# Two cross-attention layers on one core: third score group written behind the second, four maxima a layer, inverse root in eight steps, engines in another order

## Chip, cores and metric

The kernel runs on one core of a Trainium2 chip. The metric is the device time of one execution in microseconds, the median over several runs. The core has five engines with an instruction stream each: PE (TensorE, matrix products; PEld are its weight loads), DVE (VectorE), ACT (ScalarE), POOL (GpSimd) and SP (SyncE, which here issues all transfers). Products land in PSUM, eight banks of 512 floats on each of 128 partitions; an engine waits for another on semaphores.

## What is computed

Two cross-attention layers in turn, on 64 batches of 256 positions and 320 channels, 20 heads of 16. Layer 0 attends to 77 text tokens. Layer 1 attends to 73 text tokens and, with another softmax, to 4 image tokens, whose scores are raised by the cosine between what the head has read from the text and each image token. Cut to what matters:

```python
# layer 0
q, k, v = heads(x @ Wq.T), heads(text @ Wk.T), heads(text @ Wv.T)
x = merge(softmax(q @ k.T * D ** -0.5) @ v) @ Wo.T + bo + x
...
# layer 1
probs_t = softmax(q @ k_t.T * D ** -0.5)
text_out = probs_t @ v_t
qsem = l2norm(probs_t @ text_ehs)
fused = q @ k_ip.T * D ** -0.5 + 0.5 * (qsem @ l2norm(ip_ehs).T)
ip_out = (softmax(fused) * spatial_mask) @ v_ip
x = merge(text_out + ip_out) @ W_out + b_out + x
```

## The kernel before, in words

A first part (`keys_and_values`) computes keys, values and Gram matrices of all batches and stores them to HBM. The second part (`attention`) is a software pipeline over the 64 batches, written out in full: iteration i runs, on each engine, a fixed list of steps, and the step `1u3/4` is step u, part 3, of layer 1 for batch i-4. The lists are the strings of `ORDER`, one for each engine; nothing else sets the order. An engine works through its list strictly in that order, so a step that waits holds all behind it.

One batch and layer takes these steps; the engine is in brackets. q: query projection in high and low half-precision parts (PE, then ACT `q_high`, DVE `q_low`). s: scores with queries on the partitions, only to find their maxima (PE `scores`, L958 and L965; DVE `maxima`, L1184). The 20 heads lie in three groups of columns: two of 8 heads (c = 0, 1) and a third of 4 (c = 2). m: the maxima turned (PE L974, ACT `mt`). t: the scores again, with tokens on the partitions and the maximum subtracted by a product with a selector `sel` (PE `turned_scores`, L997 and L1000; ACT exponentials L1122). a: probabilities times values (PE L1017; ACT reads the sums, L1130). o: output projection (PE L933, L936; DVE L1277). Layer 1 alone has h and b (the exponentials split in two, ACT and POOL), u (times the Gram matrix, PE L1033), w (DVE L1206), n (square norms, PE L1045, ACT `nst`), i (image scores, PE L1061, ACT L1148), y (the image softmax, 21 short DVE steps L1224 to L1259 with one exponential on ACT, step f, L1154) and p (image attention, PE L1071, DVE L1266). xh and xl (POOL) split the input of a layer. SP moves the norms through HBM (ns, nl) ahead of y, the probabilities (ps, pl) ahead of p, inverse denominators (rw, rl) and numerators (sh) ahead of the step `at` of POOL.

PSUM is shared out by the table `USES`: one line for each bank, with the uses that follow one another in it. `Turns.wait` makes the first instruction of a use wait until the use before it in each of its banks has been read. Units are numbered by pairs of banks: the scores of group c go to units s2c and s2c+1, and the third group has a use of its own, s4, over four banks. In the same way t4 is the third group of the turned scores, over four banks; y is a work area of the image softmax, in one bank.

```python
uses = [f"s{2 * c}", f"s{2 * c + 1}"] if c < 2 else ["s4"]
wait_free(pe, l, b, *uses)
```

The inverse root of y is three Newton steps of three instructions each behind a bit trick of two.

Of the kernel before, what the change touches and what calls it, by code (L numbers as in the profile page):

```python
# [151 lines left out]
]  # L152
# [521 lines left out]
def attention(nc, psum, early, x, k_dram, v_dram, g_dram, c_dram, kip_dram, vip_dram, r_dram, n_dram, s_dram, p_dram,  # L674
# [3 lines left out]
    with ExitStack() as stack:  # L678
# [487 lines left out]
        def _(dve):  # L1166
# [3 lines left out]
            def maxima(l, b, n):  # L1170
# [6 lines left out]
                b.reached(dve, f_s[l], CW, c + 1)
                if n < 4:
                    o = banks(l, f"s{n}", 2)[:, :, 0:4 * m].rearrange("p r (x t) -> p r x t", t=m)
                    dst = mneg[l][:, 2 * half:2 * half + 2, 2 * c:2 * c + 2, :].rearrange("p j x s -> p j (x s)")  # L1180
                else:
                    o = banks(l, "s4", 4)[:, :, 0:2 * m].rearrange("p r (x t) -> p r x t", t=m)
                    dst = mneg[l][:, :, 4:6, 0]
# [24 lines left out]
            def ip_softmax(l, b, k):  # L1208
# [7 lines left out]

                newton = 3
                last = newton + 3 * NEWTON
                if k:
                    b.reached(dve, s_y, STEPS, k)  # L1220
                if k == 0:
                    wait_free(dve, l, b, "y")
                    b.reached(dve, s_nl, 16, 16)
# [3 lines left out]
                elif k == 2:  # L1227
                    ins = dve.tensor_scalar(y.bitcast(I32), y.bitcast(I32), -1.0, float(MAGIC), ALU.mult, ALU.add)
                elif k < last:
                    turn, part = divmod(k - newton, 3)  # L1230
                    if part == 0:
                        ins = dve.tensor_tensor(sy[:], y, sq[:], ALU.mult)
                    elif part == 1:
                        ins = dve.tensor_tensor(sy[:], y, sy[:], ALU.mult)
                    else:
                        ins = dve.scalar_tensor_tensor(y, sy[:], -3.0 * SCALES[turn] ** 2, y, ALU.add, ALU.mult)
# [259 lines left out]
```

## Time and profile before

| | us |
|---|---|
| median of 3 runs | 2527.18 (2525.49 to 2535.39) |
| profiled execution, its own time | 2528.66 |
| its span | 2526.9 |
| PE busy | 2294.1 (91%) |
| DVE busy | 1702.7 (67%) |
| ACT busy | 1709.4 (68%) |
| POOL busy | 1596.7 (63%) |

Busy times are of the whole span; the first part of the kernel takes the first sixth of it. A span is the time from the first to the last instruction of the trace. In the order of time each row gives a start in us from the start of the span, a length, the engine, the line of the kernel, what is written and read, a count, and in brackets how long the engine was idle before it and what released it; "issue" stands where the trace shows no releaser.

### The profile page before, as it was taken

What the parts mean: (1) busy time and instruction counts of PE and PEld (TensorE: products, weight loads), DVE (VectorE), ACT (ScalarE), POOL (GpSimd) and SP (SyncE); (2) the same over time, 40 slices, a digit from 0 to 9 for tenths busy, and PEclk for the clock granted to TensorE, in tenths of its full rate; (3) what the DMA queues carried; (4) which work ended last, traced back from release to release, by engine and by line L of the source; (5) the groups of instructions that cost most, each with busy time, mean ns of one, the idle gap of its engine ahead of it and who ended that gap; (6) DMA issues with size and microseconds to landing.
All of it is one profiled execution on the core that took longest, in us unless ns stands there. A gap on an engine that the chain in (4) does not pass through costs nothing.

```text
span 2526.9 us, 90581 instructions
## 1 busy us (share of the span) xinstructions
PE 2294.1 (91%) x35896; PEld 1472.0 (58%) x35896; DVE 1702.7 (67%) x3052; ACT 1709.4 (68%) x2602; POOL 1596.7 (63%) x1056
## 2 busy tenths in 40 slices
PE   7899958999989999999999999999999999999974
PEld 5677735555555555555555555555555555555542
DVE  5534424777777777777777777777777777777763
ACT  3323326777777777777777777777777777777762
POOL 3212134767777777777777776777777776777663
PEclk9999979999999999999999999999999999999997
DMA  9678632444433343344444444343443434444331
GB/s 286 196 222 236 198 106 57 111 111 112 114 107 108 112 114 110 108 116 111 116 116 116 116 113 110 107 114 109 113 115 112 111 110 111 116 115 116 109 88 54
DMA packets 337789, 310.90 MB, mean 123 GB/s; under 512 B 180208, under 2 KB 280816, under 8 KB 337392
## 3 DMA queue, kind: packets, MB, share of 16 engines
q1 hardware_dynamic: 337392, 305.36, 42.7%
q8 instruction: 280, 4.59, 0.8%
q14 instruction: 117, 0.96, 0.1%
HBM read 164.66 MB, written 105.98 MB: 107 GB/s over the span
## 4 chain that ended last, share of the span: by engine, by line
PE 51%; DVE 9%; ACT 8%; issue 7%; DMA 4%; SPq 4%; POOL 2%; ACTq 0%; DVEq 0%; POOLq 0%
PE psum L933 18%; PE psum L1017 8%; PE psum L1033 8%; PE psum L997 5%; ACT ef L1122 5%; PE psum L936 4%; DVE mneg L1184 4%; PE psum L965 2%; DVE x L1277 2%; PE psum L1071 2%; PE psum L1000 2%; DMA x<-in_x 2%; SPq L862 2%; ACT ust L1130 1%; DVE q_low L1191 1%
## 5 line engine op out<-in xcount | busy, mean ns | idle before, releaser
L1122 ACT ACTIVATE ef<-psum 73x1024 f32<-73x1024 f32 (+1 forms) x640 | 624.5, 1016 | 265.0 <-PE psum L1000 264.1
L1345 POOL TENSOR_TENSOR e<-ef,eh 73x1024 f32<-73x1024 f32 x320 | 679.1, 2131 | 179.3 <-PE psum L1045 128.3
L1184 DVE TENSOR_REDUCE mneg<-psum 128x8 f16<-128x584 f32 (+1 forms) x640 | 465.0, 775 | 138.3 <-PE psum L958 76.4
L1206 DVE TENSOR_TENSOR e<-psum,e 73x1024 f32<-73x1024 f32 x320 | 385.5, 1205 | 92.3 <-PE psum L1033 92.3
L1017 PE MATMUL psum<-ef,values 128*32 128x256 f32 x5120 | 345.0, 387 | 15.8 <-ACT ef L1122 10.8
L1033 PE MATMUL psum<-eh,gram 128*73 128x512 f16 x1280 | 333.3, 386 | 13.2 <-DVE x L1277 1.1
L997 PE MATMUL psum<-q_high,keys 32*73 32x256 f16 (+2 forms) x6144 | 325.1, 259 | 21.6 <-ACT ef L1122 19.1
L1137 ACT ACTIVATE eh<-ef 73x1024 f16<-73x1024 f32 x320 | 329.4, 1049 | 1.6
L1307 POOL TENSOR_TENSOR ust<-ust,rb 128x768 f32<-128x768 f32 x128 | 233.2, 1822 | 102.8 <-DMA ust<-ust 83.4
L1312 POOL TENSOR_TENSOR al<-ust,ah 128x768 f16<-128x768 f32 x128 | 210.1, 1641 | 89.5 <-ACT ah L1160 89.5
L1130 ACT ACTIVATE ust<-psum 128x512 f32<-128x512 f32 x384 | 215.1, 595 | 75.4 <-PE psum L1017 75.3
L997 PEld LDWEIGHTS psum<-q_high,keys 32*73 32x73 f16 (+1 forms) x6144 | 181.4, 110 | 127.2 <-issue 42.0
L933 PE MATMUL psum<-ah,wo 128*128 128x256 f16 x1280 | 194.6, 275 | 32.3 <-issue 19.6
L1302 POOL TENSOR_TENSOR xl<-x,xh 128x768 f16<-128x768 f32 x127 | 209.1, 1647 | 19.0 <-POOL xh L1295 0.9
L1017 PEld LDWEIGHTS psum<-ef,values 128*32 128x32 f32 x5120 | 135.6, 109 | 130.1 <-issue 31.1
L1295 POOL CAST xh<-x 128x768 f16<-128x768 f32 x127 | 104.7, 824 | 161.0 <-DMA x<-in_x 116.9
L1000 PE MATMUL psum<-mt,sel 32*73 32x256 f16 (+3 forms) x3072 | 202.7, 251 | 0.0
L997 PE MATMUL psum<-q_low,keys 32*73 32x256 f16 (+3 forms) x3072 | 202.6, 251 | 0.0
L1191 DVE SCALAR_TENSOR_TENSOR q_low<-psum,q_high 128x640 f16<-128x640 f32 x128 | 104.7, 818 | 142.8 <-ACT q_high L1104 142.8
L1033 PEld LDWEIGHTS psum<-eh,gram 128*73 128x73 f16 x1280 | 123.8, 115 | 120.6 <-DVE x L1277 26.7
L1045 PE MATMUL psum<-e,pick 128*32 128x256 f32 x2560 | 166.7, 389 | 1.2 <-DVE e L1206 1.2
L1089 ACT ACTIVATE res<-x,bias 128x256 f32<-128x256 f32 x320 | 140.9, 499 | 39.0 <-DVE outt L1277 24.1
(165 smaller groups left out, 4439.1 us busy)
## 6 DMA issues: line engine op xcount, KB each, us to landing
rb<-r_dram SPq DMA_DIRECT2D x128, 384.0 KB, 3.8
keys<-k_dram SPq DMA_DIRECT2D x128, 231.0 KB, 4.1
values<-v_dram SPq DMA_DIRECT2D x128, 192.5 KB
x<-in_x SPq DMA_DIRECT2D x64, 384.0 KB, 3.3
ust<-ust SPq DMA_DIRECT2D x512, 48.0 KB, 2.4
v_dram<-vst SPq DMA_DIRECT2D x64, 320.0 KB
out<-outt SPq DMA_DIRECT2D x64, 320.0 KB, 2.2
k_dram<-kst SPq DMA_DIRECT2D x32, 616.0 KB, 3.9
```

The costliest lines, as they stand in the source:

```text
L933: mm = pe.matmul(o[:, c * S:(c + 1) * S], a, data[:, k, :], **at_ends)
L997: pe.matmul(o, keys(l, low, c)[rows, e, 0:n], q[rows, cols], start=(low == 0 and q is qh[l]), stop=False)
L1000: mm = pe.matmul(o, sel[rows, 2 * c + e, 0:n], mt[l][rows, 0:many], start=False, stop=True)
L1017: mm = pe.matmul(row(l, f"a{c}")[j * SLOT:(j + 1) * SLOT, r * S:(r + 1) * S], va[l][:, h, :], e, start=True, stop=True)
L1033: mm = pe.matmul(banks(l, f"u{k}", 2)[0:n, r, :], gm[:, half, :], e, start=(half == 0), stop=(half == 1))
L1122: act.activation(ef[l][0:m, unit_heads(n), :].rearrange("t h s -> t (h s)"), src, ACT.Exp, scale=SM).then_inc(s_exp[l], 1)
L1130: act.activation(ust[l][:, b.parity(), :, c, :], src, ACT.Copy).then_inc(s_u[l], 1)
L1137: act.activation(eh[0:m, unit_heads(k), :], ef[1][0:m, unit_heads(k), :], ACT.Copy, scale=0.5)\
L1184: dve.tensor_reduce(dst, o, AX_X, ALU.max, negate=True).then_inc(s_max[l], 1)
L1206: dve.tensor_tensor(rest, banks(l, f"u{k}", 2)[0:m, :, :], rest, ALU.mult).then_inc(s_wr, 1)
L1307: pool.tensor_tensor(at(l, b), at(l, b), rb[l][:], ALU.mult).then_inc(s_at[l], 1)
L1345: pool.tensor_tensor(e2[0:m, k, :, :], ef[1][0:m, unit_heads(k), :], eh[0:m, unit_heads(k), :], ALU.subtract).then_inc(s_e2, 1)
```

## The change

The third group of scores loses its own step and its own banks. It is issued right behind the second (c = 1), into columns 4n to 6n of the same four banks. So there are two score steps a layer instead of three, and four maxima instead of five: two of 2 x 2 columns of heads and halves, then two of 2 x 3. The maxima of the third group lie elsewhere in `mneg`, and the selector product picks them with another row of `sel` and, for the second half, from other columns of `mt`; number and size of the products are the same.

The inverse root is one cubic step of five instructions and one Newton step of three, eight for nine. The wait for the bank of y moves from its first instruction, which doesn't touch the bank, to the second.

All five orders and the bank table are new. In the new table 1i shares a bank with 0a2 and 1u3; y shares one with 0a1; 0o takes banks of t4; 1o's bank goes to 0t1, the second unit of 0t0.

```diff
-RD_READ = 4 + 3 * NEWTON
+MAXIMA = 4
+CUBIC = 8.0 / 3
+ROOT_STEPS = 8
+RD_READ = 4 + ROOT_STEPS
...
 ORDER = {
...
     "dve": """
...
+        1y11/4 1y12/4 1y13/4 1y14/4 1y15/4 1y16/4 1y17/4 1y18/4 1y19/4 1ql/2 1s0/2 1s1/2 1s2/2 1s3/2 1w3/3
...
 USES = [
...
+    "0a1/1 1u3/3 0q/0 0s3/0 1t4/2 1y/3",
...
-    READ = {"q": ("ql", 1, 1), "s": ("max", UNITS, None), "m": ("mt", 1, 1), "t": ("exp", UNITS, None),
+    READ = {"q": ("ql", 1, 1), "s": ("max", MAXIMA, None), "m": ("mt", 1, 1), "t": ("exp", UNITS, None),
...
-                uses = [f"s{2 * c}", f"s{2 * c + 1}"] if c < 2 else ["s4"]
+                uses = [f"s{2 * c}", f"s{2 * c + 1}"]
...
-                if c == 2:
-                    for j in range(NJ):
-                        rows = slice(j * SLOT, (j + 1) * SLOT)
-                        o = banks(l, "s4", 4)[:, j, 0:2 * n].rearrange("p (e t) -> p e t", e=2)
-                        mm = pe.matmul(o, qh[l][rows, 2 * S:PW], keys(l, 0, c)[rows, :, 0:n], start=True, stop=True)
-                    mm.then_inc(f_s[l], 1)
-                    return
...
+                if c == 1:
+                    for j in range(NJ):
+                        rows = slice(j * SLOT, (j + 1) * SLOT)
+                        o = banks(l, uses[j // 2], 2)[:, j % 2, 4 * n:6 * n].rearrange("p (e t) -> p e t", e=2)
+                        mm = pe.matmul(o, qh[l][rows, 2 * S:PW], keys(l, 0, 2)[rows, :, 0:n], start=True, stop=True)
                 mm.then_inc(f_s[l], 1)
...
-                        mm = pe.matmul(o, sel[rows, 2 * c + e, 0:n], mt[l][rows, 0:many], start=False, stop=True)
+                        k, lead = (2 * c + e, 0) if c < 2 else (2 * c, e * many)
+                        mm = pe.matmul(o, sel[rows, k, 0:n], mt[l][rows, lead:lead + many], start=False, stop=True)
...
+                many = 2 + c
+                o = banks(l, f"s{n}", 2)[:, :, 0:2 * many * m].rearrange("p r (x t) -> p r x t", t=m)
+                dst = mneg[l][:, 2 * half:2 * half + 2, 2 * c:2 * c + many, :].rearrange("p j x s -> p j (x s)")
                 dve.tensor_reduce(dst, o, AX_X, ALU.max, negate=True).then_inc(s_max[l], 1)
...
+                cubic, newton = 3, 8
+                last = newton + 3
...
+                if k == 1:
+                    wait_free(dve, l, b, "y")
...
+                elif k in (cubic, newton):
+                    ins = dve.tensor_tensor(sy[:], y, sq[:], ALU.mult)
+                elif k == cubic + 1:
+                    ins = dve.tensor_tensor(fs, y, sy[:], ALU.mult)
+                elif k == cubic + 2:
+                    ins = dve.scalar_tensor_tensor(sy[:], fs, -10.0 / 3, sy[:], ALU.add, ALU.mult)
+                elif k == cubic + 3:
+                    ins = dve.tensor_tensor(sy[:], y, sy[:], ALU.mult)
+                elif k == cubic + 4:
+                    ins = dve.scalar_tensor_tensor(y, sy[:], 5.0, y, ALU.add, ALU.mult)
```

Three places of the order, line numbers of each kernel its own (the new one's stand a few lines lower or higher).

First PE, from the image attention of layer 1 (1p) to its output projection (1o), before: L965 and L958 are scores of layer 0 (0s0, 0s1, 0s2), L1045 the square norms, L997 the first rows of the turned scores 1t1 and 1t2, L1033 is 1u0, L1017 is 1a0.

```order
L1071 MATMUL psum<-pt,vb 128x256 x3
L1045 MATMUL psum<-e,pick 32x256 x8
L965 MATMUL psum<-keys,q_high 128x2x77 x8
L1045 MATMUL psum<-e,pick 32x256 x12
L965 MATMUL psum<-keys,q_high 128x2x77 x8
L997 MATMUL psum<-q_high,keys 73x256 x4
...
L1033 MATMUL psum<-eh,gram 73x512 x4
L997 MATMUL psum<-q_high,keys 73x128 x4
...
L1017 MATMUL psum<-ef,values 32x256 x8
L958 MATMUL psum<-keys,q_high 128x154 x4
L933 MATMUL psum<-ah,wo 128x256 x4
```

And of the change:

```order
L1069 MATMUL psum<-pt,vb 128x256 x3
L1043 MATMUL psum<-e,pick 32x256 x12
L957 MATMUL psum<-keys,q_high 128x2x77 x8
L1043 MATMUL psum<-e,pick 32x256 x8
L957 MATMUL psum<-keys,q_high 128x2x77 x8
L963 MATMUL psum<-keys,q_high 128x154 x4
L994 MATMUL psum<-q_high,keys 73x256 x4
...
L1031 MATMUL psum<-eh,gram 73x512 x4
L1015 MATMUL psum<-ef,values 32x256 x8
L994 MATMUL psum<-q_high,keys 73x128 x4
...
L932 MATMUL psum<-ah,wo 128x256 x4
```

0s0 stands behind three square-norm units instead of two, the third group directly behind 0s1, and 1a0 ahead of 1t2.

Second PE, from the first score step of layer 1 (1s0, L965) to the Gram product 1u3 (L1033), before: between them 0a1, 1s1, then 1a2 and 0a2 (x8 together), the third group 1s2 (L958) and the image scores 1i (L1061).

```order
L965 MATMUL psum<-keys,q_high 128x2x73 x8
L1017 MATMUL psum<-ef,values 32x256 x8
L965 MATMUL psum<-keys,q_high 128x2x73 x8
L1017 MATMUL psum<-ef,values 32x256 x8
L958 MATMUL psum<-keys,q_high 128x146 x4
L1061 MATMUL psum<-q_high,kipb 32x256 x2
...
L1033 MATMUL psum<-eh,gram 73x512 x4
```

And of the change:

```order
L957 MATMUL psum<-keys,q_high 128x2x73 x8
L1015 MATMUL psum<-ef,values 32x256 x12
L957 MATMUL psum<-keys,q_high 128x2x73 x8
L963 MATMUL psum<-keys,q_high 128x146 x4
L1059 MATMUL psum<-q_high,kipb 32x256 x2
...
L1015 MATMUL psum<-ef,values 32x256 x4
L1031 MATMUL psum<-eh,gram 73x512 x4
```

0a2 now stands with 0a1 (x12) ahead of 1s1, and 1a2 behind 1i.

Third DVE, from the read of 0o (written to x) to the low query part of layer 1 (q_low), the change alone:

```order
L1279 SCALAR_TENSOR_TENSOR x<-psum,res 128x768
...
L1226 TENSOR_TENSOR sy<-psum,sq 96x64
L1236 TENSOR_TENSOR sy<-psum,sy 96x64
L1238 SCALAR_TENSOR_TENSOR psum<-sy,psum 96x64
L1201 TENSOR_TENSOR e<-psum,e 73x1024
L1241 SCALAR_TENSOR_TENSOR psum<-psum,rd 96x64
L1244 SCALAR_TENSOR_TENSOR psum<-den,psum 96x256
...
L1254 TENSOR_REDUCE psum<-psum 96x64
...
L1261 TENSOR_TENSOR pip<-psum,fm 96x256
L1186 SCALAR_TENSOR_TENSOR q_low<-psum,q_high 128x640
```

Before, the whole inverse root stood ahead of the read of 0o, around the read of 1o, and only the eight steps from the product with `den` on behind it; now seven more short steps stand behind it, the product 1w2 between them, and the read of 1o stands behind the first step alone.

## Rows read from the trace of the kernel before

**Rows 1.** Busy time by stretch: length, busy us (instructions) of PE, PEld, DVE, ACT, POOL; PEclk, DMA

```profile
1300.00:1600.00 300.00, 281.10 (x4708) 175.06 (x4699) 223.10 (x397) 229.20 (x339) 215.81 (x148) 1.00 0.41 114
```

**Rows 2.** One line's instructions (image attention, step 1p), whole run: first and last start

```profile
L1071 PE MATMUL psum<-pt,vb x384: 374/478/789, 465.2 to 2514.0; 32*128 32x256 f32 x192
```

**Rows 3.** Order of time on PE, one period: start, length, instructions, idle before and releaser

```profile
1303.58 0.61 PE L933 MATMUL psum<-xh,wq 128*128 128x256 f16 x4
...
1307.86 0.31 PE L965 MATMUL psum<-keys,q_high 32*128 32x146 f16 x8 [0.21 <-ACT ef L1122]
...
1310.86 0.29 PE L1061 MATMUL psum<-q_high,kipb 128*32 128x256 f16 x3 [0.16 <-ACT ust L1130]
...
1311.31 1.06 PE L1033 MATMUL psum<-eh,gram 128*73 128x512 f16 x4
...
1316.69 0.71 PE L1071 MATMUL psum<-pt,vb 32*128 32x256 f32 x6
...
1318.54 0.32 PE L965 MATMUL psum<-keys,q_high 32*128 32x154 f16 x8
...
1320.68 0.32 PE L965 MATMUL psum<-keys,q_high 32*128 32x154 f16 x8 [0.39 <-DVE mneg L1184]
1320.85 0.31 PE L997 MATMUL psum<-q_high,keys 32*73 32x256 f16 x4
...
1323.22 0.25 PE L997 MATMUL psum<-q_high,keys 32*73 32x128 f16 x4 [0.19 <-ACT ef L1122]
...
1324.04 1.07 PE L1017 MATMUL psum<-ef,values 128*32 128x256 f32 x16 [0.17 <-ACT ef L1122]
...
1325.34 0.61 PE L933 MATMUL psum<-ah,wo 128*128 128x256 f16 x4
...
1332.82 1.05 PE L1033 MATMUL psum<-eh,gram 128*73 128x512 f16 x4
...
1335.81 0.61 PE L933 MATMUL psum<-xh,wq 128*128 128x256 f16 x4
```

**Rows 4.** Waits of the whole run: us in total, times, longest

```profile
PE psum L933 <- issue: 19.6, 13, 1.7
```

**Rows 5.** Order of time, all engines, around one of those waits

```profile
1066.94 1.25 DVE L1224 TENSOR_SCALAR sq<-n 96x64 f32<-96x64 f32 x1 [0.91 <-DMA n<-n_dram]
...
1069.39 0.81 DVE L1277 SCALAR_TENSOR_TENSOR outt<-psum,res 128x640 f32<-128x640 f32 x1
...
1070.31 0.60 PE L933 MATMUL psum<-ah,wo 128*128 128x256 f16 x4 [1.69 <-issue]
```

**Rows 6.** Order of time on ACT, same period as rows 3

```profile
1302.38 0.38 ACT L1154 ACTIVATE psum<-psum 96x256 f32<-96x256 f32 x1
...
1310.21 1.09 ACT L1130 ACTIVATE ust<-psum 128x512 f32<-128x512 f32 x2 [0.32 <-PE psum L1017]
1311.50 0.38 ACT L1148 ACTIVATE sipst<-psum 96x256 f32<-96x256 f32 x1 [0.20 <-PE psum L1061]
```

**Rows 7.** Order of time on DVE, same period

```profile
1300.45 0.41 DVE L1242 SCALAR_TENSOR_TENSOR psum<-den,psum 96x256 f32<-96x256 f32 x1
...
1304.59 0.42 DVE L1259 TENSOR_TENSOR pip<-psum,fm 96x256 f32<-96x256 f32 x1
...
1317.52 0.96 DVE L1266 TENSOR_TENSOR ust<-psum,ust 128x768 f32<-128x768 f32 x1 [1.40 <-PE psum L1071]
...
1319.13 1.49 DVE L1184 TENSOR_REDUCE mneg<-psum 128x8 f16<-128x616 f32 x2
```

**Rows 8.** Groups of DVE instructions by form, 1000 to 2000 us: busy us, mean ns, idle before

```profile
L1184 DVE TENSOR_REDUCE mneg<-psum 128x8 f16<-128x616 f32 x151 | 114.8, 793 | 52.7 <-PE psum L958 37.8 <-PE psum L965 14.8
L1184 DVE TENSOR_REDUCE mneg<-psum 128x8 f16<-128x584 f32 x155 | 107.4, 757 | 14.6 <-PE psum L965 14.4 <-issue 0.2
```

**Rows 9.** Order of time on POOL, same period as rows 3

```profile
1312.03 1.65 POOL L1302 TENSOR_TENSOR xl<-x,xh 128x768 f16<-128x768 f32 x1
```

**Rows 10.** Transfers by tile, the store of norms (n_dram), 1000 to 2000 us

```profile
DMA to landing us min/median/max: 1.7/2.5/4.0
```

More of the change, by code:

```diff
@@ L48 @@
 UNITS = 5
-SCALES = [1.0]
-for _ in range(NEWTON):
-    SCALES.append(-2.0 * SCALES[-1] ** 3)
-RD_READ = 4 + 3 * NEWTON
+MAXIMA = 4
+CUBIC = 8.0 / 3
+ROOT_STEPS = 8
+RD_READ = 4 + ROOT_STEPS
 SQ_READ, SEM_READ, SIP_READ, STEPS = 1, RD_READ + 1, RD_READ + 2, RD_READ + 7
@@ L125 @@
     "pe": """
-        1s1/3 1a2/4 0a2/2 1s2/3 1i/3 1u3/4 1m/3 1u4/4 1t0/3 0q/1 1p/5 1n0/4 1n1/4 0s0/1 1n2/4 1n3/4 1n4/4
-        0s1/1 1t1/3 1u0/3 1t2/3 1a0/3 0s2/1 1o/5 0m/1 1u1/3 0o/2 0t0/1 1u2/3 1a1/3 0t1/1 1q/2 0t2/1 0a0/1
-        1s0/2 0a1/1""",
+        1q/2 0t2/1 0a0/1 1s0/2 0a1/1 0a2/1 1s1/2 1i/2 1a2/3 1u3/3 1m/2 1u4/3 1t0/2 0q/0 1p/4 1n0/3 1n1/3
+        1n2/3 0s0/0 1n3/3 1n4/3 0s1/0 1t1/2 1u0/2 1a0/2 1t2/2 1o/4 0m/0 1u1/2 0o/1 0t0/0 1u2/2 1a1/2 0t1/0""",
     "act": """
-        0a1/2 1a2/4 0a2/2 1i/3 1m/3 0r/1 1t0/3 1t1/3 1h0/3 0q/1 1h1/3 1g/5 1n/4 1t2/3 1t3/3 1t4/3 1a0/3 0g/2
-        1h2/3 1h3/3 0m/1 1r/3 0t0/1 0t1/1 1f/4 1h4/3 0t2/1 0t3/1 1q/2 0t4/1 1a1/3 0a0/1""",
+        1f/4 1q/2 0t4/1 0a0/1 0a1/1 0a2/1 1i/2 1a2/3 1m/2 1t0/2 1t1/2 1h0/2 0q/0 0r/0 1g/4 1n/3 1h1/2 1t2/2
+        1t3/2 0g/1 1a0/2 1t4/2 1h2/2 1h3/2 0m/0 1r/2 1h4/2 0t0/0 0t1/0 1a1/2 0t2/0 0t3/0""",
     "dve": """
-        1s1/3 1s2/3 1s3/3 1s4/3 1w3/4 0d/2 1d/4 1w4/4 1p/5 0ql/1 0s0/1 0s1/1 0s2/1 0s3/1 1w0/3 0s4/1 1y0/4
-        1y1/4 1y2/4 1y3/4 1y4/4 1y5/4 1o/5 1y6/4 1y7/4 1y8/4 1w1/3 1y9/4 1y10/4 1y11/4 1y12/4 0o/2 1y13/4
-        1y14/4 1y15/4 1y16/4 1w2/3 1y17/4 1y18/4 1y19/4 1y20/4 1ql/2 1s0/2""",
+        1y11/4 1y12/4 1y13/4 1y14/4 1y15/4 1y16/4 1y17/4 1y18/4 1y19/4 1ql/2 1s0/2 1s1/2 1s2/2 1s3/2 1w3/3
+        0d/1 1w4/3 1p/4 0ql/0 0s0/0 0s1/0 0s2/0 0s3/0 1w0/2 1y0/3 1o/4 1d/3 1y1/3 1y2/3 1y3/3 1w1/2 0o/1
+        1y4/3 1y5/3 1y6/3 1y7/3 1y8/3 1y9/3 1y10/3 1w2/2""",
     "pool": """
-        1c/3 1kb/2 1b0/3 1al/5 1b1/3 0at/2 0al/2 1b2/3 1b3/3 1xh/2 1xl/2 1b4/3 1vb/4 1at/4 0xh/0 0xl/0""",
+        1kb/2 1b4/3 1at/4 0xh/0 0xl/0 1b0/2 1c/2 1al/4 0at/1 0al/1 1b1/2 1b2/2 1vb/3 1xh/1 1xl/1 1b3/2""",
     "sp": """
-        1ds/4 0ds/2 1v/3 1g/3 0k/1 0rw/2 0sh/2 0rl/2 1ns/4 1nl/4 1d/4 1st/5 1rw/4 1rl/4 0v/1 1ss/3 1k/2 1c/2
-        1sh/4 1ps/4 1sl/3 1vi/3 0x/0 1pl/4""",
+        0v/1 1ss/3 1k/2 1rw/4 1rl/4 1sh/4 0x/0 1sl/3 1ps/4 0ds/1 0k/0 1vi/3 1pl/4 0rw/1 1c/2 1g/2 1v/2 0rl/1
+        0sh/1 1ns/3 1ds/3 1nl/3 1st/4 1d/3""",
 }
 USES = [
[8 rows of a table removed]
[8 rows of a table added]
 ]
@@ L970, in turn_max @@
                 wait_free(pe, l, b, "m")
-                b.reached(pe, s_max[l], UNITS, UNITS)
+                b.reached(pe, s_max[l], MAXIMA, MAXIMA)
                 o = row(l, "m").bitcast(F16)
@@ L1176, in maxima @@
                 b.reached(dve, f_m[l], 1, 0)
[L1177 to L1183, printed above, removed]
+                b.reached(dve, f_s[l], 2, c + 1)
+                many = 2 + c
+                o = banks(l, f"s{n}", 2)[:, :, 0:2 * many * m].rearrange("p r (x t) -> p r x t", t=m)
+                dst = mneg[l][:, 2 * half:2 * half + 2, 2 * c:2 * c + many, :].rearrange("p j x s -> p j (x s)")
                 dve.tensor_reduce(dst, o, AX_X, ALU.max, negate=True).then_inc(s_max[l], 1)
@@ L1228, in ip_softmax @@
                     ins = dve.tensor_scalar(y.bitcast(I32), y.bitcast(I32), -1.0, float(MAGIC), ALU.mult, ALU.add)
[L1229 to L1236, printed above, removed]
+                elif k in (cubic, newton):
[8 more added lines that the diff above has]
+                    ins = dve.scalar_tensor_tensor(y, sy[:], 5.0, y, ALU.add, ALU.mult)
+                elif k == newton + 1:
+                    ins = dve.tensor_tensor(sy[:], y, sy[:], ALU.mult)
+                elif k == newton + 2:
+                    ins = dve.scalar_tensor_tensor(y, sy[:], -3.0 * CUBIC ** 2, y, ALU.add, ALU.mult)
                 elif k == last:
                     b.reached(dve, s_rd[1], 1, 1)
-                    ins = dve.scalar_tensor_tensor(y, y, EPS / SCALES[NEWTON], rd[1][:, b.parity(), :], ALU.mult, ALU.min)
+                    ins = dve.scalar_tensor_tensor(y, y, EPS / (-2.0 * CUBIC ** 3), rd[1][:, b.parity(), :], ALU.mult, ALU.min)
                 elif k == last + 1:
```

3 lines of the change are left out of this document (removed), and 15 rows, old and new, of the table USES.

## The prediction

> **What bounds the kernel now.** I read the busy table by stretch first, then the order of time on PE over one period, then the waits, then what the other engines do at each PE wait.
>
> In a stretch of the steady part TensorE is busy 281 of 300 us at a granted clock of 1.00 (the 2.4 GHz level), VectorE 223, ScalarE 229, GpSimd 216 [rows 1]. So the PE stream sets the time, and only its 6 per cent of gaps can be won without removing matmuls. The 64 batches pass one landmark (step 1p) between 465.2 and 2514.0 us [rows 2]: 2048.8 / 63 = 32.5 us a period on average, fill and drain included. An undisturbed period is shorter: 1q starts at 1303.58 and again at 1335.81, 32.23 us [rows 3]. The difference has a visible part: 13 times in the run PE waits some 1.5 us ahead of an output projection, 19.6 us in all, with no releaser named [rows 4].
>
> One of them in detail [rows 5]: the first softmax step of the image tokens (sq) waits 0.91 us for the norms' DMA and then takes 1.25 us; five short steps follow it, 0.24 each; the read of 1o (outt) begins only at 1069.39 and ends at 1070.20; PE's 0o starts at 1070.31. 0o was waiting for a PSUM bank that 1o still held, with DVE late because the softmax stood ahead of 1o's read.
>
> **The change, part by part.** No matmul is removed: the four of the third score group remain, with the same rows and columns. Time can come only from waits. I follow the three pieces of a period [rows 3], each counted from its own first matmul, in the new order.
>
> *1q to 1p, before 13.11 us.* The wait of 1s0 for the exponential of 0t2 stays: same neighbours on ACT and PE, so 1s0 starts at 4.28 as before. New order: 0a1 (4.51 to 5.52), 0a2 (half as many matmuls, to 6.02), 1s1 with the third group behind it (0.25 + 0.17, to 6.44). 1i now takes the bank of 0a2, so it waits for ACT's read of 0a2, and no more for that of 1a2. A read takes 0.60 [rows 6], and begins 0.2 behind its matmuls: 6.22 to 6.82, 1i at 6.87, 0.43 lost. Then 1a2 (0.5), and 1u3, which now takes the bank of 1i: from 1i's first matmul to the end of ACT's read it is 1310.86 to 1311.88 [rows 3, 6], 1.02 us, so 1u3 starts at 7.95 instead of 7.73 [rows 3]. The rest is unchanged: **0.22 lost**, 13.33.
>
> *1p to 1o, before 8.65 us.* Three square-norm units, not two, now cover DVE's read of 1p: it ends 1.79 behind 1p's start [rows 3, 7], 0s0 was free to start at 1.85, and is now reached at 2.14, with no wait. Before, 0s1 wrote into the banks of the second maximum and waited until both were taken. Now its first pair of banks is that of the first maximum alone. Two maxima take 1.49 [rows 7], the first some 0.79: started at 2.57 it is done at 3.36, and PE arrives at 3.39. So 0s1 runs 3.42 to 3.84 instead of waiting to 3.99. 1t1 pays a part back: it takes the banks of the second maximum (done 4.06), and starts at 4.12 (before 4.16). 1u0 waits for the third maximum, which is the first large one. Its size, 128x924, is not in the trace. A reduction of 584 elements takes 757 ns, one of 616 takes 793 [rows 8]: 1.1 ns an element, so 1.14 us. Bounds: 0.79 (no dearer than now) and 1.59 (two of today's). With 1.14 it ends near 5.16, 1u0 starts at 5.22, 0.1 lost; with 1.59, 0.17 more in the period, as 1a0's wait then shrinks; with 0.79 nothing is lost. 1a0 moves ahead of 1t2. It waits for the exponential that today holds 1t2, 2.37 behind 1t1 [rows 3]: 6.49. It runs 1.0 us, under which the next exponential ends (3.19 behind 1t1, 7.31), so 1t2 at 7.49 finds it done, and the separate third group with its waits (1a0 and 0s2 took 1.30 for 1.17 of work) is gone. 1o starts at 8.06: **0.59 gained**.
>
> *1o to the next 1q, before 10.47 us.* Same steps in the same order. 1u2 still waits for DVE's read of 0o; 1q still follows its read banks and POOL's xl. **Nothing.**
>
> Period 13.33 + 8.06 + 10.47 = 31.86, that is 0.37 less; over some 62 full periods 23 us.
>
> *The late norms.* 0o now takes banks left by the 1t4 exponential, and 1o's bank goes on to the second pair of 0t0, 3.8 us behind 1o's end. 1o's read can be two microseconds late without holding PE. I count 16 of the 19.6 us [rows 4], the rest kept for reads that come later still.
>
> *What costs nothing* (spare times by the same walk, so estimates). Four maxima for five and one Newton step less save DVE under 0.5 us a period, and DVE idles a quarter of the time [rows 1]. If that cover went, DVE would be the bound with 24 us of work in 31.9. On ACT the residual 0r moves behind 0q, 0g ahead of the 1a0 read and the 1t4 exponential: 0m, which waits for the latter, has about 0.9 us to spare. On POOL 1c stands behind 1b0 and the 1b1 difference behind 0al; both results are needed over 2 us later. On SP, 0ds, 0k, vi and pl move behind 1ps, and 1c, 1g, 1v behind 0rw; each lands 1.5 us or more ahead of its reader. The restriction is on x and the numerators, see the second rival.
>
> **Sum:** 23 + 16 = 39 us off the profiled execution, 2528.66 us with a span of 2526.9. The runs' median, 2527.18, lies 1.5 lower, so **2488 us**; the forecast's own range is 2474 to 2506 (third maximum between its bounds: +11 and -6; waits of 0.1 us each wrongly read at three places: 18 us).
>
> **Rivals.**
> *A. The image softmax becomes PE's wait.* Its work area now shares a bank with 0a1, so all of it must be over at 4.51 behind 1q. From the last reading of 0o (just ahead of 1u2, 2.99 us before 1q [rows 3]) DVE does seven short steps (0.24 each, five fill the gap ahead of outt [rows 5]), a product of 1.2, one more short step, and the last eight. Those took 1300.45 to 1305.01 with a product between [rows 7], which covered the hand to ACT and back (0.38 and two hand-offs of 0.1); without it about 4.1. Sum 1.7 + 1.2 + 0.25 + 4.1 = 7.3, so the area is free at 4.3: 0.2 to spare, where before the last step ended at 1305.01, 1.4 behind 1q [rows 7], a microsecond ahead of need. If the chain runs 0.6 us longer (the exponential on ACT is now directly behind two large ones and ahead of 1q), PE waits 0.4 more a period: 25 us given back, 2513. For it: the small margin. Against: every duration in it is measured.
>
> *B. Slower: SP's queue.* The numerator moves 1sh and the load of x stand on SP behind the store of 1o, four other moves, and 1rl, which waits until the stored inverses have reached HBM. In my walk x is split at about 10.1 behind 1q, 0.8 ahead of 0q (before: POOL's xl ends at 1313.68, 10.10 [rows 9]). If stores land late, everything behind 1rl slips: the store of norms took from 1.7 to 4.0, median 2.5 [rows 10]. A slip beyond 0.8 makes 0q wait; beyond 1.4 all of the gain is gone (0.63 a period with the late norms). At 2.3 (4.0 less 1.7) PE waits 1.5 a period, 1.13 over today's 32.23: 70 us, less the 16, 2581; at 2.0, 2562. Against: such a landing would have to come in nearly every period.
> The Trainium skill ("Perfetto Trace Analysis", section "DMA Instruction — HWDGE (DVE, Sync)") says that the last descriptor's semaphore write waits for the data write to be confirmed, which "can cause a surprisingly long delay especially when the write target is HBM". That speaks for B, as the change puts more behind such a wait; by it the time would be B's. The trace agrees that landings spread, by 2.3 us [rows 10], and their median speaks for the forecast.
>
> *C. No change.* PE's gaps fill elsewhere and the removed waits only show later ones: 2520 to 2530. For it: PE is 94 per cent busy already [rows 1]. Against: a wait with a removed cause [rows 5].
>
> **Numbers.** A run of this kernel tells 0.5 per cent (13 us) from no change. Forecast 0.64, A 0.15, B 0.11, C 0.10. A lies just on the faster side of 2514.5, and half of it beyond: faster 0.64 + 0.08 = 0.72; same 0.07 + 0.10 = 0.17; slower 0.11. The range reaches from below the forecast's own, for cheaper waits, to A and part of C: 2472 to 2524; B, half of C and a rest below stay outside.
>
> **What would show it.** A period of 31.8 to 31.9 between two 1q without disturbance; 1u3 near 7.95 behind 1q and later than before; 1o near 8.06 behind 1p, without a wait for a maximum at 0s1, with short ones at 1t1 and 1a0; large maxima of 1.07 to 1.14 us; no unnamed wait of 1.5 us ahead of 0o. Wrong if 0a1 waits for the softmax's last step (A), 0q for POOL's xl with SP's rl late (B), or if the period stays at 32.2 (C).

## The result, and the profile after

The change made the kernel slower: **2579.74 us** (median of 4 runs, 2575.01 to 2582.58) against 2529.11 of before in the same comparison, a ratio of **1.0196 (95 per cent interval 1.0168 to 1.0223)**. The forecast of 2488 and its range, 2472 to 2524, missed; the time is near that of rival B (2581 was its price for a landing 2.3 us late).

Line numbers have moved: in after, L932 and L935 are the projections (0q, 1q, 0o, 1o), L957 and L963 the scores, L994 and L998 the turned scores, L1015 `a`, L1031 `u`, L1059 1i, L1069 1p. The page of after, its span, two busy lines, the chain that ended last (by engine, then by line, the head of a long line left as it is), and POOL's product of numerators and inverses (1at, 0at):

```profile
span 2580.8 us, 90259 instructions
...
PE 2269.5 (88%) x35896; PEld 1471.3 (57%) x35896; DVE 1677.6 (65%) x2860; ACT 1713.7 (66%) x2602; POOL 1591.9 (62%) x1056
...
DMA 22%; PE 21%; SPq 20%; issue 8%; DVE 6%; POOL 6%; ACT 3%; DVEq 0%; ACTq 0%; POOLq 0%
...
L1309 POOL TENSOR_TENSOR ust<-ust,rb 128x768 f32<-128x768 f32 x128 | 232.6, 1818 | 256.1 <-DMA ust<-ust 255.7
```

The same two lines on the page of before:

```profile
PE 51%; DVE 9%; ACT 8%; issue 7%; DMA 4%; SPq 4%; POOL 2%; ACTq 0%; DVEq 0%; POOLq 0%
...
L1307 POOL TENSOR_TENSOR ust<-ust,rb 128x768 f32<-128x768 f32 x128 | 233.2, 1822 | 102.8 <-DMA ust<-ust 83.4
```

Before, half of the chain was TensorE's. Now transfers and SP's issuing make 42 per cent of it, and TensorE 21: the kernel is no longer bound by the PE stream. Busy time in the stretch of [rows 1] says the same, 268.8 of 300 us where it was 281.1:

```profile
1300.00:1600.00 300.00, 268.80 (x4574) 169.24 (x4573) 213.36 (x357) 223.28 (x330) 208.54 (x142) 0.99 0.39 109
```

Waits of after between 1000 and 2000 us (total, times, longest):

```profile
POOL ust L1309 <- DMA ust<-ust: 101.8, 43, 5.0
...
PE psum L932 <- POOL xl L1304: 38.3, 28, 3.0
...
PE psum L1069 <- DMA pt<-p_dram: 6.6, 7, 1.5
```

0q waits for POOL's xl in nearly every period; the step 1t0 ahead of it lasts 2.40 us in the median of 30 periods, 1.00 in its shortest form. In 62 periods 1.4 us each are 87 of the 93 us between this span and 2488. The chain of waits shows the whole loop, one period long (start, length, what):

```profile
1312.51 0.84 DVE outt L1279
1313.37 0.36 SPq L909
...
1313.83 0.56 SPq L852
...
1316.16 0.51 SPq L820
...
1316.71 0.77 SPq L888
...
1317.52 0.45 SPq L813
...
1318.02 0.71 SPq L868
...
1318.77 3.33 DMA r_dram<-rd
...
1322.16 0.58 SPq L874
...
1322.86 0.59 SPq L861
...
1325.44 0.53 SPq L805
...
1326.60 4.83 DMA p_dram<-pip
1331.44 4.27 DMA pt<-p_dram
...
1335.84 0.73 PE psum L1069 x6
...
1346.40 0.84 DVE outt L1279
1347.25 0.36 SPq L909
```

DVE's read of 1o lets SP store the output (L909); behind it in SP's list come four moves (L852), values, s_dram and keys (L820, L888, L813), the store of inverses 1rw (L868), whose landing 1rl (L874) waits for, the numerators 1sh (L861, four of 0.6), x (L805) and the image probabilities, on which 1p waits; 1p leads to the next 1o. Every link waits for the one ahead, and the loop takes 33.88 us from L909 to L909. The next turn of the same chain leaves SP at the numerators and goes over POOL's 1at and xl to 0q: two ends of one queue. x stands in that queue too, and in 14 of 29 periods between 1000 and 2000 us the trace names its landing, not the numerators', as what POOL waited for last ahead of 0q's xh and xl.

Before, the hold at 1rl was shorter. SP in one period, the store of inverses and the spread, first of before, then of after:

```profile
1329.20 1.41 SPq L869 DMA_DIRECT2D r_dram<-rd  x2
1331.90 0.58 SPq L875 DMA_DIRECT2D rb<-r_dram  x1
```

```profile
1318.02 1.39 SPq L868 DMA_DIRECT2D r_dram<-rd  x2
1322.16 0.58 SPq L874 DMA_DIRECT2D rb<-r_dram  x1
```

In before rl leaves 1.29 us behind the end of rw; in after it is 1322.16 - 1319.41 = 2.75, and 2.74 in the median of 27 periods (1.76 to 3.66; both counted on SP's order of time between 1000 and 2000 us, as all holds below).

### The profile page after: what moved, and what is told of

The parts are those of the page before. It is cut to its first block, busy times and chain, and to the rows that moved or that the text cites. A ratio compares the mean times of both kernels' runs of the same rounds, so it can differ in the third digit from the quotient of the medians.

```text
span 2580.8 us, 90259 instructions
## 1 busy us (share of the span) xinstructions
PE 2269.5 (88%) x35896; PEld 1471.3 (57%) x35896; DVE 1677.6 (65%) x2860; ACT 1713.7 (66%) x2602; POOL 1591.9 (62%) x1056
## 4 chain that ended last, share of the span: by engine, by line
DMA 22%; PE 21%; SPq 20%; issue 8%; DVE 6%; POOL 6%; ACT 3%; DVEq 0%; ACTq 0%; POOLq 0%
PE psum L932 8%; DMA r_dram<-rd 8%; SPq L861 5%; SPq L852 5%; DMA ust<-ust 4%; PE psum L994 3%; DMA p_dram<-pip 3%; DMA pt<-p_dram 3%; PE psum L1015 3%; ACT ef L1120 3%; POOL xl L1304 2%; DMA x<-in_x 2%; PE psum L935 2%; DVE outt L1279 2%; DVE mneg L1179 2%
## 5 line engine op out<-in xcount | busy, mean ns | idle before, releaser
L1179 DVE TENSOR_REDUCE mneg<-psum 128x8 f16<-128x616 f32 (+3 forms) x512 | 450.0, 930 | 11.5 <-PE psum L963 1.4
L994 PE MATMUL psum<-q_high,keys 32*73 32x256 f16 (+2 forms) x6144 | 324.6, 258 | 37.0 <-DVE mneg L1179 19.9
L1015 PE MATMUL psum<-ef,values 128*32 128x256 f32 x5120 | 344.9, 386 | 12.7 <-ACT ef L1120 12.5
L1031 PE MATMUL psum<-eh,gram 128*73 128x512 f16 x1280 | 332.3, 385 | 26.2 <-issue 10.1
L1128 ACT ACTIVATE ust<-psum 128x512 f32<-128x512 f32 x384 | 221.2, 593 | 82.8 <-PE psum L1015 78.5
L994 PEld LDWEIGHTS psum<-q_high,keys 32*73 32x73 f16 (+1 forms) x6144 | 179.5, 110 | 151.0 <-issue 62.4
L932 PE MATMUL psum<-xh,wq 128*128 128x256 f16 x1024 | 159.5, 279 | 79.7 <-POOL xl L1304 68.6
L1268 DVE TENSOR_TENSOR ust<-psum,ust 128x768 f32<-128x768 f32 x64 | 61.3, 958 | 248.7 <-PE psum L1069 248.7
L1304 POOL TENSOR_TENSOR xl<-x,xh 128x768 f16<-128x768 f32 x127 | 209.0, 1646 | 18.7 <-POOL xh L1297 0.4
L1015 PEld LDWEIGHTS psum<-ef,values 128*32 128x32 f32 x5120 | 138.0, 109 | 138.7 <-ACT ef L1120 43.0
L1031 PEld LDWEIGHTS psum<-eh,gram 128*73 128x73 f16 x1280 | 124.2, 115 | 152.5 <-issue 42.1
L932 PE MATMUL psum<-ah,wo 128*128 128x256 f16 x1280 | 195.8, 276 | 10.8 <-POOL al L1314 10.8
L998 PE MATMUL psum<-mt,sel 32*73 32x256 f16 (+3 forms) x3072 | 201.1, 251 | 0.0
L994 PE MATMUL psum<-q_low,keys 32*73 32x256 f16 (+3 forms) x3072 | 200.9, 251 | 0.0
L1158 ACT ACTIVATE ah<-ust 128x768 f16<-128x768 f32 x128 | 107.4, 839 | 81.8 <-POOL ust L1309 41.8
```

The source lines that it names most:

```text
L932: mm = pe.matmul(o[:, c * S:(c + 1) * S], a, data[:, k, :], **at_ends)
L994: pe.matmul(o, keys(l, low, c)[rows, e, 0:n], q[rows, cols], start=(low == 0 and q is qh[l]), stop=False)
L1015: mm = pe.matmul(row(l, f"a{c}")[j * SLOT:(j + 1) * SLOT, r * S:(r + 1) * S], va[l][:, h, :], e, start=True, stop=True)
L1031: mm = pe.matmul(banks(l, f"u{k}", 2)[0:n, r, :], gm[:, half, :], e, start=(half == 0), stop=(half == 1))
L1128: act.activation(ust[l][:, b.parity(), :, c, :], src, ACT.Copy).then_inc(s_u[l], 1)
L1304: pool.tensor_tensor(xl[l][:], xin[l][:], xh[l][:], ALU.subtract).then_inc(s_xl[l], 1)
```

## The experiments

Fifteen more kernels ran. Unless something else is said, each is the changed kernel with SP's list altered; ratios are to the kernel before, with 95 per cent intervals.

| run | us | ratio |
|---|---|---|
| e1, SP's order of before | 2601.6 | 1.0267 (1.0230 to 1.0305) |
| e2, 1rw first | **2489.7** | **0.9842 (0.9815 to 0.9868)** |
| e3, before with 1rw late | 2807.1 | 1.1091 (1.1060 to 1.1121) |
| e4, e5, code alone, two numberings | 2591.6, 2548.9 | 1.0249, 1.0083 (1.0050 to 1.0116) |
| e6, 1sh ahead of 1rl | 2499.9 | 0.9892 (0.9862 to 0.9922) |
| e7, 1rw 1rl first | 2550.3 | 1.0085 (1.0057 to 1.0114) |
| e8, e2 with 0g behind 1t4 | 2525.1 | 0.9986 (0.9972 to 1.0000) |
| e9, e10, e11, e2 with small moves | 2490.2, 2494.4, 2494.1 | 0.9850, 0.9867, 0.9858 |
| e12, e13, 1rw behind 0v or 1ss alone | 2554.3, 2641.1 | one execution each, no interval |
| e14, 1rw behind 1k alone | 2562.6 | 1.0108 (1.0074 to 1.0142) |
| e15, 1rw behind 0v and 1k | 2522.3 | 0.9948 (0.9930 to 0.9966) |

### Where SP's queue holds: e2, e1, e3

```diff
-  0v/1 1ss/3 1k/2 1rw/4 1rl/4 1sh/4 0x/0 1sl/3 ...
+  1rw/4 0v/1 1ss/3 1k/2 1rl/4 1sh/4 0x/0 1sl/3 ...
```

> The changed kernel with one word moved on SP: the store of inverses 1rw from behind the loads of values and keys (0v, 1ss, 1k) to ahead of them. Theory S: 1rl no longer waits (in the changed kernel 2.4 to 2.8 us from the end of 1rw's issue to 1rl's), so 1rl, 1sh, x, ps follow about 1.5 to 2.5 us earlier; 0q's wait of 1.5 us mostly goes: 2490 to 2530 us. If the delay is instead the numerators' own landing behind the spread inverses (3 us behind their issue instead of 1.7), part of the wait stays: 2530 to 2555. Rival P: 2570 to 2585, no change.

One word moved gives 2489.7 us, 90 less than the change, and the time that had been forecast. SP of this run, one period: the three loads and stores now fill the hold, rl leaves without one, and x 6.8 us behind the last of the four moves where it was 9.4 (medians):

```profile
1310.47 2.29 SPq L852 DMA_DIRECT2D den<-ust  x4
1312.80 1.41 SPq L868 DMA_DIRECT2D r_dram<-rd  x2
1314.25 0.48 SPq L820 DMA_DIRECT2D values<-v_dram  x1
...
1315.54 0.46 SPq L813 DMA_DIRECT2D keys<-k_dram  x1
1316.10 0.58 SPq L874 DMA_DIRECT2D rb<-r_dram  x1
```

0q's wait is gone (its total between 1000 and 2000 us fell from 38.3 to 0.3), and PE is the chain's largest part again, with 41 per cent. PE of the same run, one period, answering to [rows 3]; its starts are used in the comparison below:

```profile
1318.69 0.61 PE L932 MATMUL psum<-xh,wq 128*128 128x256 f16 x4
...
1325.54 0.29 PE L1059 MATMUL psum<-q_high,kipb 128*32 128x256 f16 x3 [0.53 <-ACT ust L1128]
...
1326.66 1.03 PE L1031 MATMUL psum<-eh,gram 128*73 128x512 f16 x4 [0.17 <-issue]
...
1332.06 0.71 PE L1069 MATMUL psum<-pt,vb 32*128 32x256 f32 x6
...
1335.43 0.32 PE L957 MATMUL psum<-keys,q_high 32*128 32x154 f16 x8
...
1336.13 0.31 PE L994 MATMUL psum<-q_high,keys 32*73 32x256 f16 x4 [0.32 <-DVE mneg L1179]
...
1350.52 0.61 PE L932 MATMUL psum<-xh,wq 128*128 128x256 f16 x4
```

In e1 SP got the list of before (1ds behind 0k):

```diff
+  0v/1 1ss/3 1k/2 1c/2 1sh/4 1ps/4 1sl/3 1vi/3 0x/0 1pl/4 ... 1st/4 1rw/3 1rl/3
```

> The changed kernel with SP's order of the kernel before (the same sequence of transfers, lags adapted; only the move of layer 1's denominators, 1ds, stands behind 0k, as ACT reads 1a2 later in the new order). Theory S, the loss is SP's order: the store of inverses 1rw again stands directly behind the store of the output, ahead of the loads of values and keys, and the numerators 1sh no longer directly behind the spread 1rl. PE's wait for POOL's xl ahead of 0q (about 1.5 us a period) goes, the period falls from 33.7 to 31.9 to 32.2 us, the time to 2480 to 2505 us. Rival P, POOL's order or the banks make 0q late whatever SP does: the wait stays, 2560 to 2585 us. Rival Q, both share it: 2520 to 2550.

It missed: 2601.6. The hold is 1.29 again, yet now x stands behind 1ps, which waits for DVE's image probabilities, and these come later in the new DVE order. Waits of e1, 1000 to 2000 us:

```profile
SPq L899 <- DVE pip L1261: 54.8, 30, 3.0
PE psum L932 <- POOL xl L1304: 50.9, 29, 3.3
```

So the order of before is no remedy: the new order of DVE needs a new one on SP, and in the one that it had the place of 1rw alone was worth 90 us. Nearly the converse, in the kernel before; it moves 1d, 1c and x as well:

```diff
-  1st/5 1rw/4 1rl/4 0v/1 1ss/3 1k/2 1c/2 1sh/4 1ps/4 ...
+  1st/5 1d/4 0v/1 1ss/3 1k/2 1rw/4 1rl/4 1sh/4 0x/0 ...
```

> The converse: the kernel before, its code, banks and other orders unchanged, with SP's new sequence from the store of the output on: 1st, 1d, 0v, 1ss, 1k, 1rw, 1rl, 1sh, x, sl, ps. Theory S: 1rl is held until the inverses land behind values and keys, 1at and with it xl come late, PE waits ahead of 0q as in the changed kernel: 2550 to 2600 us. Rival P: 2520 to 2535, as before.

Slower, but by 278 us, where 20 to 70 were expected: the hold is 2.76 as in after, and 0q waits for xl in 23 periods between 1000 and 2000 us (25.2 us in all). The direction fits; as more than 1rw moved, this run doesn't show that 1rw alone did it. Of the size, five times that of the change, a part is TensorE's clock: between 500 and 2400 us the granted clock is 0.97 of 2.4 GHz where it was 1.00 before, with stretches at 1.2 GHz, at most some 57 us (an estimate, 0.03 of 1900). The rest I didn't follow.

### The code alone: e4, e5

The code of the change (larger maxima, root of 8 steps) under the orders and banks of before, without the steps that no longer exist. The diff of e5 against e4 on DVE:

```diff
-  1y9/4 1y10/4 1y11/4 1y12/4 0o/2 1y13/4 1y14/4 1y15/4 1y16/4 1w2/3 1y17/4 ...
+  1y9/4 1y10/4 1y11/4 0o/2 1y12/4 1y13/4 1y14/4 1y15/4 1w2/3 1y16/4 ...
```

> The code of the change alone: third group written behind the second, four maxima, root in eight steps, with all orders and the bank table of the kernel before (less the removed steps). By the walk the removed step gives back what 1i (waits for the read of 1a2, which now comes 0.15 later) and 1t1 (0.25 later, behind the longer 0s1) lose, and the late norms stay: 2515 to 2535 us, no change. If the merged maxima themselves cost (rival T: large reductions dearer than 1.14 us hold the banks): 2540 to 2560. If the code alone gains, 2490 to 2515.

> The code of the change under the orders and banks of before, as in the run before it, but with the softmax steps behind the root one place earlier, so that 1w2 again stands between the fourth- and third-last of the softmax's steps, where it stood before. Theory N (that run's loss was the 0.83 us that 1q waited for 1w2 in 29 of 31 periods, a matter of numbering): the wait is gone and some 48 us with it, 2535 to 2555; what stays above 2529 is the larger third maximum (1u0 0.42, 1u3 0.36 of wait). Rival M (the wait merely shows DVE late by the larger maxima): 1q or 1u2 goes on waiting, 2575 or more.

e4 (2591.6) wasn't what it was meant to be: the root is one step shorter, so the same number stands for the next step, and 1w2 stood behind the one that waits for ACT. e5 puts that right: 2548.9, as expected there. What remains is the larger third maximum, which PE awaits at 1u0 and 1u3 under the old banks. Waits between 1000 and 2000 us, of e4 for 1w2, of e5 for the maximum:

```profile
PE psum L932 <- DVE e L1201: 23.9, 29, 0.8
```

```profile
PE psum L1031 <- DVE mneg L1179: 24.0, 61, 0.8
```

The code alone thus loses 0.8 per cent; the gain of e2 comes only with the new orders and banks.

### What makes the store land late: e7, e12 to e15

In each, 1rl stands directly behind 1rw, so that the hold is the landing, and what is ahead of 1rw changes.

```diff
+  e7:  1rw/4 1rl/4 0v/1 1ss/3 1k/2 1sh/4 ...
+  e12: 0v/1 1rw/4 1rl/4 1ss/3 1k/2 1sh/4 ...
+  e13: 1ss/3 1rw/4 1rl/4 0v/1 1k/2 1sh/4 ...
+  e14: 1k/2 1rw/4 1rl/4 0v/1 1ss/3 1sh/4 ...
+  e15: 0v/1 1k/2 1rw/4 1rl/4 1ss/3 1sh/4 ...
```

> The change with 1rw and 1rl both at the head of SP's list, ahead of 0v, 1ss and 1k, so that nothing large stands ahead of the store in the queue and nothing hides its landing. Theory Q (the store of inverses lands later when values, s_dram and keys, 520 KB, stand ahead of it in the queue): the hold at rl falls from 2.4 to 2.75 us to about 1.3, numerators leave 1.0 to 1.5 earlier than in the changed kernel, 2490 to 2515. Rival L (the landing is 2.4 to 2.75 whatever stands ahead): the hold stays at 2.4 or more, numerators leave about as late as now, 2565 to 2585.

> The change with 1rw and 1rl behind 0v alone: 192 KB of values ahead of the store, not 520 KB. Theory Q (the landing grows with what stands ahead of the store in the queue): the hold at rl lies between 1.29 (nothing ahead) and 2.74 (520 KB), at 1.7 to 2.3 us. Rival (any load ahead costs the same, or only the store to s_dram or the keys directly ahead matter): 2.7, or 1.3.

> The change with 1ss alone ahead of 1rw and 1rl (0v and 1k behind them). If the store to s_dram ahead delays the store of inverses (two stores to HBM one after the other): hold at rl 2.0 us or more. If it is the keys: 1.3 to 1.4. Keys late as in the runs with 1k behind 1rl: 1s0 waits for them, 2545 to 2560.

> The change with 1k alone ahead of 1rw and 1rl (0v and 1ss behind them). If the keys directly ahead delay the store of inverses: hold 2.0 us or more; if only the store to s_dram does: 1.3 to 1.4. With the keys early 1s0 does not wait for them. Theory K (the 2550 of the runs with 1rl near the head was the late keys alone): 2488 to 2505. Rival (numerators or x still late): 2530 or more, with 0q waiting for POOL's xl.

> The change with 0v and 1k ahead of 1rw and 1rl, and 1ss behind them: all that stands ahead in the changed kernel but the store to s_dram. If loads ahead delay the store only together, or the keys do: hold 2.0 us or more, and 0q waits for xl in part of the periods, 2510 to 2560. If only the store to s_dram does: hold 1.3 to 1.4, keys early, 2490 to 2505.

| directly ahead of 1rw | hold at 1rl, median (shortest to longest), us | last packet ahead over, us | last packet of the inverses over, us |
|---|---|---|---|
| nothing (e7) | 1.29 (1.27 to 2.82) | | 0.90 |
| values (e12) | 1.38 (1.29 to 3.63) | 0.53 | 0.96 |
| keys (e14) | 1.30 (1.27 to 3.14) | 0.42 | 0.90 |
| store to s_dram (e13) | 1.71 (1.68 to 3.61) | 0.95 | 1.30 |
| values, keys (e15) | 1.62 (1.29 to 3.32) | 0.71 | 1.20 |
| values, s_dram, keys (after) | 2.74 (1.76 to 3.66) | 1.98 | 2.33 |

Theory Q holds at its ends: with nothing ahead the store lands as in the kernel before, and with all three 1.45 us later. My expectation of a landing in proportion to the bytes fell (192 KB of values cost 0.1), and so did that of one culprit: none of the three alone costs more than 0.42, and the three apart add up to 0.52.

Why they don't add is in the DMA packets of the traces, which can be told apart by size (values 2560 bytes, s_dram 1024, keys 1848, inverses 256). The two columns on the right give when the last of them is over, in us from the end of 1rw's issue, medians of 28 to 31 periods. In every run rl leaves 0.4 us behind the last packet of the inverses. That one ends 0.35 to 0.5 behind the last packet ahead, but not before 0.9, its time with nothing ahead. So the store waits for what is left of the queue ahead of it, and a transfer that is over by 0.5 costs next to nothing. In after the packets of s_dram are over at 1.38 and those of the keys behind them at 1.98. Why the keys, over at 0.42 without s_dram and values ahead, drain so late stays open.

The times of e7, e12, e13 and e14 missed what was expected too, for another reason: the loads behind rl now came late. In e7 and e12 1s0 waits for its keys (1000 to 2000 us; of e12 the row), and in e13, where values and keys both stand behind, PE stands ahead of the products with values (second row):

```profile
PE psum L957 <- DMA keys<-k_dram: 38.4, 27, 4.2
```

```profile
PE psum L1015 <- issue: 35.2, 15, 4.1
```

In e14 the keys are early and the values late. Their load leaves at 1018.96, and 0a0, next on PE, stands 2.88 us:

```profile
1018.96 0.53 SPq L820 DMA_DIRECT2D values<-v_dram  x1
```

```profile
1023.67 1.59 PE L1015 MATMUL psum<-ef,values 128*32 128x256 f32 x16 [2.88 <-issue]
```

No releaser is named there, but it is the values: the semaphore of their landing has its last update 0.2 us ahead of 0a0. The same holds for each wait above 0.5 us at L1015 between 1000 and 2000 us, 22 in e14, 28 in e13 and 13 in e7. Theory K, that the keys alone were the rest, fell. e15, with both loads early, is at 2522, its hold between the two that were expected, and 0q waits for xl in 13 periods of 31. Hence the hold has to be covered, not only shortened: e2 puts three issues into it, of which values and keys can't wait.

### Numerators in the hold: e6

```diff
-  ... 1rw/4 1rl/4 1sh/4 0x/0 ...
+  ... 1rw/4 1sh/4 1rl/4 0x/0 ...
```

> The change with one swap on SP: 1sh ahead of 1rl, so that the issue of the numerators (2.48 us) fills the hold and x and the numerators no more stand behind 1rl; the store of inverses keeps its late place. Theory S (what costs is the time at which numerators and spread inverses reach POOL's 1at): rl leaves about where it leaves now, and lands 4.2 later, near 1326.4 on the clock of the changed kernel, against numerators at 1327.0: POOL then waits for the inverses instead, half of the loss is won back, 2530 to 2560. Rival X (x alone sets it): x leaves 2.5 us earlier, all is won back, 2485 to 2500.

2499.9, the upper end of what X gave and 30 below S: rl leaves about where it did, and POOL waits for the spread inverses as S says (55.2 us in 31 periods), but of 0q's wait 4.7 us in 9 periods are left. S was wrong on the price: 1at starts at 6.29 behind 1q where it was 7.59, and x lands at 7.83 where it was 9.16 (medians); 1.3 us each are nearly enough. As both came earlier, the run doesn't tell x from the numerators.

### Faster than both? e8 to e11

e2 leaves waits on PE: 0m for the 1t4 exponential (11.4 us in 17 of 31 periods) and 1i. On ACT, and on PE:

```diff
   e2:  1t2/2 1t3/2 0g/1 1a0/2 1t4/2 1h2/2       1s1/2 1i/2 1a2/3 1u3/3
+  e8:  1t2/2 1t3/2 1a0/2 1t4/2 0g/1 1h2/2
+  e9:  1t2/2 1t3/2 1a0/2 0g/1 1t4/2 1h2/2
+  e10:                                          1s1/2 1a2/3 1i/2 1u3/3
+  e11: as e9                                    as e10
```

> The run with 1rw at the head of SP's list, and on ACT 0g behind the 1t4 exponential, not ahead of the read of 1a0: in that run ACT stood 2.7 us at 0g waiting for POOL, with the read and the exponential ready behind it, and 0m on PE waited for the exponential (11.4 us in 17 of 31 periods, up to 1.8). If that is a wait of its own: 0m's wait goes, 1o to 0m falls from a mean of 2.76 to 2.4, 15 to 22 us in all, 2468 to 2476. If the image branch (0g, POOL's product behind it, 0o) is the limit anyway: the wait moves to 0o and the time stays at 2487 to 2492.

> The run with 1rw first, and on ACT 0g between the read of 1a0 and the 1t4 exponential: POOL's product, for which 0g waits, comes no earlier, so 0g keeps its time; only the read (0.58 us) is done while ACT would stand, and the exponential ends some 0.45 us earlier. If 0m's wait (11.4 us in 17 of 31 periods of that run) is a matter of this read: it falls by 0.3 to 0.45 in each of these periods, 7 to 15 us over the run, 2474 to 2484. If 0g itself slips behind the read (it is ready earlier than the read in some periods), 0o waits for POOL's al as in the run with 0g behind the exponential, by up to 0.5 a period: 2487 to 2500.

> The run with 1rw first, and on PE 1a2 ahead of 1i: 1i waited 0.53 us for ACT's read of 0a2 in every period, and 1a2 (0.5 to 0.65 us) can run meanwhile, if the maximum whose bank it takes is taken by then. If so: 1i's wait goes, 1u3, which needs the read of 1i, moves from 8.0 to 7.7 or 7.8 behind 1q, 0.2 to 0.3 us a period, 12 to 19 us, 2470 to 2480. If the second maximum (0.79 and 1.07 us from 1s0 and 1s1) holds 1a2 instead: the same wait stands one place earlier, 2485 to 2500.

> Both of the two: sum of what the two single moves bring, 2455 to 2470 if both come off; if the waits are shared with another engine (GpSimd's or VectorE's chain as the next bound) less than the sum.

None beat e2. In e8 0m's wait is gone and two new ones stand behind it (1000 to 2000 us): 0t0 waits for DVE's product of 1u1, and 0o for POOL's split of what 0g copied:

```profile
PE psum L994 <- DVE e L1201: 14.5, 31, 0.5
PE psum L932 <- POOL al L1314: 9.9, 31, 0.6
```

In e9 0m's wait fell to 2.3 us in 5 periods, and 7.2 us in 19 came at 0t0 in its place; in e10 and e11 1i waits no more, and 1u3 waits 18.7 us in 31 periods (no releaser is named; by the bank table it is the bank of 1i), so that it starts the same 1.88 us behind 1s1's last four matmuls in e2 and e10. Both waits were ACT's: moved, not removed.

## Why the prediction was wrong

**The PE stream: right.** In e2, where nothing else holds it, medians over 31 periods between 1000 and 2000 us: 1q to 1p 13.33 us (forecast 13.33), 1p to 1o 7.93 (8.06), 1o to 1q 10.56 (10.47), sum 31.82 (31.86); the misses of the last two, 0.1 each, cancel. In after the second piece is 7.93 as well. By steps: 1i waited 0.53 (0.43), 1u3 came 7.97 behind 1q (7.95); 0s1 did not wait; 1t1 started 4.07 behind 1p (4.12). The large maxima, unseen in the trace of before, cost 1.11 and 1.07 (1.14); groups of after by form:

```profile
L1179 DVE TENSOR_REDUCE mneg<-psum 128x12 f16<-128x924 f32 x128 | 136.7, 1110 | 0.2 <-issue 0.2
L1179 DVE TENSOR_REDUCE mneg<-psum 128x12 f16<-128x876 f32 x128 | 131.0, 1065 | 9.8 <-PE psum L963 1.4
```

**The late norms: right.** The unnamed waits of 1.5 us ahead of 0o [rows 4] are in no list of waits of after or e2.

**Rival A: did not come.** No 0a1 waits for the softmax.

**"0m has about 0.9 us to spare": wrong, and small.** 0g holds ACT up to 2.7 us until POOL is done (38.8 us in 31 waits of e2), and 0m waits. Of e2's mean period, 32.08 us, this is the largest part above its shortest, 31.58.

**The failed step: SP's walk**, "In my walk x is split at about 10.1 behind 1q, 0.8 ahead of 0q". It writes down no term for the hold at 1rl; 10.1 is about what the order of after gives with the landings of before, which were taken as the transfers' own. In after the hold is 2.74 instead of 1.29, as three transfers were put ahead of the store: 1.45 us. Behind the spread of 384 KB the numerators of 1at land 2.05 us behind the end of their issue (before 1.80), and x 3.7 behind its issue (before 3.3): 0.25 to 0.4 us more. That makes 1.7 to 1.9 us; measured are 2.1, as xl ends 12.16 behind 1q in the median of 30 periods (in the turn of the chain behind the one shown 1366.52 less 1354.10, 12.42) instead of 10.1. That is rival B's mechanism and nearly its wait, 1.4 us a period where the price of 2581 had 1.5; its chance, 0.11, rested on "such a landing would have to come in nearly every period", which treated the spread of landings [rows 10] as chance. It was set by the order: the same store lands in 1.29 or in 2.74 by what SP issued ahead of it.

The Trainium skill's sentence on stores to HBM ("Perfetto Trace Analysis", section "DMA Instruction — HWDGE (DVE, Sync)"), cited beside B, puts the delay into the confirmation of the write. By that sentence the time would have been B's, and so it came; but the trace doesn't bear out the reason. From the last packet of the inverses to rl it is 0.4 us in before, e7 and after alike, and the 1.45 us lie ahead of it, in the packets queued in front.

The ends of the forecast's own range, 2474 and 2506, aren't the sums of the terms named for them (11, 6 and 18 us); nothing else rested on them.

## What to carry to other kernels

A landing time read in one order of the queue isn't a constant of the transfer: when a change puts other transfers ahead of a store that something waits for, price the wait again, with both ends, and follow the queue behind it around the whole period to the step that started it. Put a store on whose landing a later issue waits as early as its data allow, and the issues that can't be late into the wait, rather than ahead of the store. When nine tenths of a long order table are right, one word can still turn the sign; a run with that one word moved back tells it.

## What the runs showed that I had not expected

- The landing of two stores of 24 KB: 1.29 to 1.38 us behind the end of their issue with nothing, values or keys ahead, 1.71 behind a store of 96 KB, 2.74 behind all three (table above). It follows the last packet queued ahead, not the sum of what each costs alone.
- 0v and 1k, loads that seem to have a whole period, have nearly none: behind 1rl they cost 61 to 73 us (both in e7, 0v in e14, against e2).
- The one-core program has a loop through SP of 33.9 us a period in after that no single engine's busy share shows: SP only issues, PE is 88 per cent busy, and neither is the longest part of the chain.
